# Signalling pairs of fp32 matmuls by a queue drain, in a four-layer graph network on one core

## The reference

```
x = layernorm(x + L0(x))     # relu(x @ W + sum over incoming edges of (x @ M)[src])
x = layernorm(x + L1(x))     # two attention layers of 4 heads
x = layernorm(x + L2(x))     # three transformer-like layers of 8 heads, with edge types
x = layernorm(x + L3(x))     # per relation: weighted sum of h[src], then a block product
```

```
L0:  agg = segment_sum(msg[edge_src], edge_dst)                      # msg = x @ M
L3:  agg = segment_sum(h[edge_src] * edge_norm[:, None], rel * N + dst)
```

## Time and profile before

| | |
|---|---|
| median of 3 runs | 7653.98 us |
| span of the profiled execution | 7518.3 us |
| median less span | 135.7 us |
| first sum of rows (stretch 853 to 1528 us) | 675 us, PEclk 0.65 |
| second sum of rows (stretch 6851 to 7493 us) | 642 us, PEclk 0.69 |
| PE busy over the span | 4867.8 us (65%) |
| DVE, ACT, POOL busy over the span | 52%, 47%, 50% |

### The profile page before, as it was taken

The page is one execution under the profiler, slowest core; times in us unless marked ns, Lnnn a source line. Parts: engine busy times, 40 slices in busy tenths (PEclk is TensorE's granted clock), DMA queues, the critical chain, the costliest instruction groups (busy, mean ns, idle before and its releaser), DMA issues. The chain is left out here.

```text
span 7518.3 us, 87581 instructions
## 1 busy us (share of the span) xinstructions
PE 4867.8 (65%) x24003; PEld 3723.3 (50%) x24003; DVE 3884.0 (52%) x9168; ACT 3561.5 (47%) x8843; POOL 3734.9 (50%) x3964
## 2 busy tenths in 40 slices
PE   4444445447775677657767886677896777796444
PEld 3444333324553445445555774555694555574332
DVE  7222222235665566756667436666545666573233
ACT  2333232224444444455555564555575555454555
POOL 1655466646663566245555235555224555314665
PEclk6555566666767677787777997777897777798676
DMA  1111233333442344255556125555325555423333
GB/s 59 47 47 47 72 93 91 92 88 108 109 109 71 102 108 110 68 174 163 172 164 161 58 97 160 166 169 166 77 68 162 165 174 167 126 79 114 93 91 91
DMA packets 392076, 841.54 MB, mean 112 GB/s; under 512 B 92953, under 2 KB 203451, under 8 KB 388163
## 3 DMA queue, kind: packets, MB, share of 16 engines
q0 software_dynamic: 209680, 603.03, 28.9%
q1 hardware_dynamic: 173696, 228.71, 9.6%
q10 hardware_dynamic: 8243, 4.30, 0.2%
HBM read 727.80 MB, written 107.96 MB: 111 GB/s over the span
## 5 line engine op out<-in xcount | busy, mean ns | idle before, releaser
L700 POOL DMA_INDIRECT ring<-tab_kv,idx_i x1392 | 1322.0, 950 | 1172.1 <-PE pp L769 578.5
L943 DVE TENSOR_TENSOR acc<-acc,pp 128x264 f32 x1576 | 670.6, 425 | 942.3 <-DMA WE<-in_L_gnn_W_E 339.3
L700 POOL DMA_INDIRECT ring<-tab_z,src_i x880 | 842.0, 957 | 541.3 <-issue 237.5
L769 PE MATMUL pp<-ring,X 128*128 128x264 f32 x2784 | 946.4, 492 | 200.1 <-issue 162.0
L1126 PE MATMUL pp<-ring,oh 128*128 128x256 f32 x1760 | 598.9, 499 | 639.7 <-DMA bb<-in_L_gnn_b 221.5
L726 PE MATMUL pq<-Qs,oht 128*128 x6816 | 813.0, 257 | 257.7 <-issue 162.8
L726 PEld LDWEIGHTS pq<-Qs,oht 128*128 128x128 bf16 x6816 | 636.2, 109 | 506.4 <-issue 320.9
L1260 DVE TENSOR_TENSOR acc<-acc,pp 128x256 f32 x880 | 370.3, 421 | 882.4 <-remote 275.8
L1126 PEld LDWEIGHTS pp<-ring,oh 128*128 128x128 f32 x1760 | 419.2, 251 | 819.8 <-issue 465.1
L769 PEld LDWEIGHTS pp<-ring,X 128*128 128x128 f32 x2784 | 629.8, 241 | 351.8 <-issue 203.4
L769 PE MATMUL pp<-ring,scratch 128*128 128x264 f32 x1760 | 648.0, 510 | 128.5 <-issue 68.2
(11 more groups left out here) (356 smaller groups left out, 8992.6 us busy)
## 6 DMA issues: line engine op xcount, KB each, us to landing
oht<-lo_row_p SPq DMA_DIRECT2D x174, 256.0 KB
tab_kv<-X SPq DMA_DIRECT2D x100, 384.0 KB
oht<-lo_row_s SPq DMA_DIRECT2D x110, 256.0 KB
drow<-in_dst SPq DMA_DIRECT2D x25, 1024.0 KB
tab_h<-hs SPq DMA_DIRECT2D x25, 1024.0 KB, 4.4
ring<-tab_kv,idx_i POOLq DMA_INDIRECT x1392
tab_kv<-room SPq DMA_DIRECT2D x50, 384.0 KB, 3.0
ring<-tab_z,src_i POOLq DMA_INDIRECT x880
```

The costliest lines, as they stand in the source:

```text
L700: nc.gpsimd.indirect_dma_start(out=ring[:, w % RW, c, :], out_offset=None, in_=table, in_offset=bass.IndirectOffsetOnAxis(ap=idx[:, w * WC ...
L769: last = nc.tensor.matmul(pp[n % NB][:, 0:W8], oh[:, w % 2, UC * n + c, :], ring[:, w % RW, UC * n + c, 0:W8], start=(c == 0), stop=(c == ...
L943: nc.vector.tensor_tensor(a, a, pp[p % NB][:, 0:W8], ALU.add).then_inc(s_acc, 1)
```

## The change

In `sum_edges`, PE's second matmul of a pair no longer carries the increment of `s_p`. A drain of PE's queue stands behind each pair, and carries it.

```
@@ -1123,9 +1123,9 @@
                             e.wait_ge(s_g[b][k], i * 32 + 32)
                             e.wait_ge(s_v, u * BODY + 2 * (k + 1))
                             for c in range(2):
-                                last = nc.tensor.matmul(bank[:, c * D:(c + 1) * D], oh[:, b, 2 * k + c, :],
-                                                        ring[:, b, k, c, :], start=True, stop=True)
-                            last.then_inc(s_p, 1)
+                                nc.tensor.matmul(bank[:, c * D:(c + 1) * D], oh[:, b, 2 * k + c, :],
+                                                 ring[:, b, k, c, :], start=True, stop=True)
+                            nc.tensor.drain().then_inc(s_p, 1)
```

## The result

The kernel with drains takes 7687.39 us (median of 8 runs, 7665.70 to 7706.11); the kernel before, run beside it, 7653.02 us (8 runs, 7634.04 to 7667.93). The ratio is 1.005 [1.0036, 1.0065]: 34 us slower (28 to 50). The forecast was + 5 us, 7659; 7687 is in the range of 8 in 10, but outside the likeliest case's own 7640 to 7669, and on the side of the slower rival.

The account below looks back on a forecast made before the run. POOL's gathers were taken to bound both sums, hiding PE's added time; POOL's later waits added 5 us, the ends and late signals 0, so 7653.98 became 7659 us, with an 8-in-10 range of 7600 to 7748.

Parts of the forecast that it names:

- the likeliest case: Whole kernel: time stays within 0.2% (15 us), predicted 7659 us, own range 7640 to 7669; chance 0.42.
- the slower rival: Ring in both sums: PE cannot rebuild its lead after a pause; 7717 us at a third of 188, 7842 full; chance 0.36.
- the two stretches: The two sums of rows, 675 and 642 us: each was to stay within 5 us.
- POOL bounds both sums: Both sums: POOL's gathers set the pace, 2.52 us a pair, 554 us a sum; 162 us are waits within PE's reach.
- A pair costs 1.24 us warm and 2.17 us cold: PE in both sums: with drains each pair stands alone, costing 0.31 us more warm, 0.39 cold, 136 to 172 us in all.
- That time is hidden by POOL's 2.52 us a pair: Both sums: the added PE time fits in PE's 639.7 us of idle time, since POOL brings pairs more slowly.
- A drain's signal is as late as the increment's: PE's signal while gathers run: the drain's increment arrives no sooner than the matmul's did, so no gain.
- the faster rival: PE's signal in both sums: the drain's signal escapes the delay; 7573 us, or 7492 with all 162 us freed; chance 0.21.
- 96 x 0.05 = 5 us for POOL's waits: POOL in both sums: each of 96 waits ends later by the drain's 0.05 us, 4.8 us in all.
- The ends cost 0: Ends of both sums: PE's last pairs stay hidden behind DVE's adds; without DVE's backlog 10 us at most.
- Nothing moves outside the sums: All other stages: no change; the prediction is wrong if the time moves by anything outside the two sums.
- The 135.7 us between median and span are unchanged: Whole kernel: the median's excess over the profiled span of 7518.3 us was taken as the same after the change.

Follow-up runs that it names:

- ring-of-two kernels: Second sum's ring cut from 4 bodies to 2, against the kernel before: 7533.42 us, ratio 0.9995; with drains in that sum too, 7544.23 us, 0.9999.
- PE's wait for itself: Both sums, no drains: PE waits for its own matmul increment before the next pair, against the kernel before: ratio 1.0006; on another chip 1.0000.

## Why the prediction was right, and where it was wrong

The time came out within the range of 8 in 10, and no step of the sum gives it: the forecast's own + 5 us is a seventh of the measured 34. The prediction named its own sign of being wrong, that the two stretches move by more than 15 us together. They moved by 48 us in the profiled pair and by some 30 on one chip. The time lies in the range because the range was made wide enough for half of the slower rival's full price; as far as the sum goes, that is luck.

- *POOL bounds both sums:* right up to the ends. Its busy time, its idle time and the ends add up to the growth of the stages.
- *A pair costs 1.24 us warm and 2.17 us cold:* nearly. It is 1.33 and 2.27; the gap from one pair to the next is 0.23 us, where the sum had 0.14 warm (load, drain and wait). No load of the next pair lies beside a running one (PEld's 0.73 starts 0.03 us before its matmuls). The Trainium skill, "PSUM — Partial Sum Buffer", section "Engine vs sequencer instructions", has a drain wait for the engine to be fully idle; the trace agrees.
- *That time is hidden by POOL's 2.52 us a pair:* shown at 6205 us, where the drains cost 0 within 0.11% in each sum. At 7541 and 7653 us POOL's pace of 2.52 us is the same and hides it only in part.
- *A drain's signal is as late as the increment's:* right, against the faster rival. Drains were held for up to 11.7 us.
- *96 x 0.05 = 5 us for POOL's waits:* this is the step that failed. It let each of POOL's waits end 0.05 us later and kept their number, and it took all 96 for waits, though 45 of them are the usual gap of 0.30 us. Measured, POOL's idle time grew by 33.5 us in the profiled pair (49.9 more put down to waits on a signal, 16.4 less to issue and the rest), with 97 idle stretches above 0.5 us in place of 65. By the estimate above perhaps half of that is the drains'; between the change and the ring-of-two kernels on one chip, POOL's idle time in the first sum is 242.2 us against 236.2 and 234.3. The forecast had noted that the drain's signal is held, and that a drain holds PE's queue, but not put the two together: a held drain stops PE in the middle of a body, so the work behind it is not done during the hold but after it. That is what the timelines suggest; no experiment shows it.
- *The ends cost 0:* wrong. They cost 12.3 us in the profiled pair, more than the bound of 10, and 8 to 9 us in the first sum alone on one chip. The bound took as many pairs left in front of PE as before (four and eight). There were 15 in each, since PE no longer runs ahead; then PE at 1.33 us a pair is behind DVE's 1.20.
- *The slower rival:* its direction is right and half of its mechanism. PE's lead is lost, and POOL's waits grew. But PEclk was 0.68 in both sums, above the 0.65 of before in the first and only just below the 0.69 in the second, and a pair time above 1.9 us did not decide it: at 6205 us the granted clock was 0.63 to 0.64 in the sums and cold pairs took 2.3 us (2.08 and a gap of 0.23), at no cost. The ring's depth has no part in POOL's pauses, and one in the ends. Its price was a third of 188, 63 us; measured were 25 and 34.
- *Nothing moves outside the sums:* can't be told from the pair of profiles, in which the stages outside differ by 98 us. On the chips at 6205 us they are 5045 to 5061 us together, in seven kernels with these gathers, drains or not.
- *The 135.7 us between median and span are unchanged:* a wrong reading, since 1.7 us lie outside the span; the profile before is of a faster execution. The sum was not hurt by it.

What stays open: whether at 7541 to 7653 us the price is due to the drain's hold on PE's queue, as the timelines suggest, or to the signal that now sits on it. The drain without a signal and PE's wait for itself would tell, and ran only on chips where the change costs nothing. The hold as a cause is read from a timeline, not shown by an experiment. Nor is it told apart from the plain pace after a hold: a row of waiting pairs takes 1.33 or 2.27 us each with drains, where DVE needs 1.20. None of the versions that do the whole work beats the kernel before by more than its interval.

## What to carry to other kernels

Leave the increment on the last matmul: a drain behind each pair buys nothing, and it cost nothing only where another engine's pace covers the pair alone (2.52 us against 1.33 to 2.27 here) and no signal comes late. Ask also what is left in front of the slowed engine when the stream ends: there nothing covers it. When a row shows that signals come late, ask what the sender does meanwhile: by these timelines a signal that can be outrun costs less than one that the sender waits on. Check whether a profile's span fits the timed runs before two profiles are held against each other; here 26 of 48 us may be the executions' own difference. And time a change of synchronization on more than one chip before it is called free; here drains in one sum gave 0.9998 and 1.0000 on one chip, and the whole change 1.0029 on another.

## What was not expected of the hardware

- **The same kernel takes 6205 us on one chip and 7541 us on another.** Each chip was used at one time only, so that it is the chip, and not the hour, is not shown. The difference lies nearly all in stages with gathers. A kernel with drains in the second sum at 6205 us, against the profile before: the sort is 604 us instead of 721 in the earlier trace rows's profile, the sums 579 and 568 instead of 688 and 643, the attention layers 584, 584, 625, 627, 628 instead of 751, 751, 854, 856, 853; the dense stages are 328, 328, 326 and 329, 329, 326. One gather's busy time is the same, 957 and 958 ns. What differs in the rows is that at 6205 us no signal is late: POOL waits for PE for 0.6 us in a second sum, and no drain is over 2.12 us in any of these kernels. What holds the signals up on the other chips no run shows.
- **Some held signals come in soon after POOL stops, and nearly as many don't.** In the profile after POOL's gather ends at 7335.17 and the held drain lets go by 7337.94, 2.8 us later; the one before ends at 7314.39 and the signal is there by 7317.07, 2.7 us later. But of the 123 drains over 2.5 us, 55 end while POOL goes on, as the one before 7331.43, and the 68 others end 0.4 to 4.0 us after its last gather. POOL's stop is thus not needed to end a hold, and since POOL stands until a signal comes, some ends would fall into its pauses anyway.
- **A pair and its drain:** 1.33 us at a granted clock of 1.00 and 2.27 us at 0.50, against 0.93 and 1.78 without; the gap of 0.23 us from one pair to the next is the same at both.
- **DVE's slow instructions are gone with drains.** The sequencer's register operations of the adds took up to 1396 ns in the kernel before (wait instructions up to 1399); after they are all alike:

```profile
L1258 DVEq EVENT_SEMAPHORE  x440: 21/21/21, 947.5 to 7637.1; - x147
...
L1260 DVEq FUSED_REGOPS  x880: 57/57/65, 948.5 to 7637.9; - x176
```

It did not help, since DVE waits for PE. At 6205 us they are alike too, in a sum without drains as well, so they go with the late signals; what made them slow is not known.
